# A recurrence, two attentions and a mixture of experts on one core: loads and splits reordered ahead of and in the recurrence, two pairs of padding memsets, a last chunk of 64 hidden rows

## The reference

```
x = x + attn(gru(cond, x))                    # x: [4, 256, 256]
x = x + ffn(adaln(x, cond))
gru:  r = sigmoid(x W_ih_r + h W_hh_r + b), z likewise, n = tanh(i_n + r * h_n)
      h = (1 - z) * n + z * h                 # 256 steps, batch 4, width 256
attn: 16 heads of width 128, causal           # W_q, W_k, W_v: 256 -> 2048
adaln: rms norm, scale and shift from cond @ W_emb; 16 heads of width 16 with
      rms norm of q and k by the gains g_q and g_k, no mask; o + o W_out
ffn:  16 experts of 176 hidden rows, the best 4 weighted, and one shared
      expert of 704 rows: silu(x W_gate) * (x W_up) @ W_down
```

## Time and profile before

| | us |
|---|---|
| median of 3 runs | 1003.25 (1001.9 to 1003.27) |
| the profiled execution | 1002.73 |
| its span | 1000.9 |
| busy: TensorE | 940.7 (94%) |
| VectorE | 694.6 (69%) |
| ScalarE | 593.7 (59%) |
| GpSimd | 581.4 (58%) |

### The profile page before, as it was taken

One profiled execution on the slowest core, in us unless ns is written; L12 is line 12 of the kernel. 1 busy time (PEld: TensorE's weight loads), 2 busy tenths in 40 slices (PEclk: granted clock), 3 DMA queues, 4 the chain that ended last, 5 costly groups with the idle time before them and its releaser, 6 DMA issues. The chain is left out here.

```text
span 1000.9 us, 37739 instructions
## 1 busy us (share of the span) xinstructions
PE 940.7 (94%) x15017; PEld 756.7 (76%) x15017; DVE 694.6 (69%) x2755; ACT 593.7 (59%) x2051; POOL 581.4 (58%) x1274
## 2 busy tenths in 40 slices
PE   3899999999999999998999999877999999999997
...
GB/s 370 47 15 24 25 25 25 20 19 25 25 25 24 20 19 25 25 32 96 72 73 72 73 127 41 21 41 1 2 2 5 60 134 112 111 125 118 125 112 44
DMA packets 79803, 58.99 MB, mean 59 GB/s; under 512 B 64886, under 2 KB 70776, under 8 KB 79116
## 3 DMA queue, kind: packets, MB, share of 16 engines
...
## 5 line engine op out<-in xcount | busy, mean ns | idle before, releaser
L577 POOL COPY gp<-hq 128x16 f16<-128x16 f16 x256 | 68.1, 266 | 152.8 <-DVE hq L541 152.7
L1988 PE MATMUL gu<-wq_part 128*128 128x512 f16 x660 | 151.5, 379 | 0.0
L617 POOL TENSOR_TENSOR q_part<-q_raw,q_part 128x64 f16<-128x64 f32 x237 | 113.1, 477 | 19.2
L352 PE MATMUL gq<-gp,wq_part 128*128 128x64 f16 x1422 | 120.6, 242 | 0.0
L280 PE MATMUL gr<-hq,w_one 128*128 128x4 f16 x2048 | 118.1, 166 | 0.0
L336 PE MATMUL gq<-gp,raws 128*128 128x64 f16 x1440 | 115.3, 237 | 0.0
L1988 PEld LDWEIGHTS gu<-wq_part 128*128 128x128 f16 x660 | 64.5, 98 | 66.5 <-issue 0.4
L2065 ACT ACTIVATE h_hi<-hT 128x512 f16<-128x512 f32 x56 | 35.3, 630 | 129.3 <-DVE hT L2135 129.3
L390 ACT ACTIVATE r_scan<-gr 128x8 f32<-128x8 f32 x256 | 46.1, 180 | 111.0 <-PE gr L280 110.9
L615 POOL CAST q_part<-q_raw 128x64 f16<-128x64 f32 x237 | 110.0, 464 | 0.4
L352 PEld LDWEIGHTS gq<-gp,wq_part 128*128 128x128 f16 x1422 | 94.5, 132 | 0.0
...
## 6 DMA issues: line engine op xcount, KB each, us to landing
...
```

The costliest lines, as they stand in the source:

```text
L352: mm = pe.matmul(q_bank[t % 2][:, 0:B * QB].rearrange("p (b t) -> p b t", b=B), wq_part[:, w, c, j * P:(j + 1) * P], gp[:, g, j, :, h * QB ...
L577: nc.gpsimd.tensor_copy(gp[:, :, :, :, t].rearrange("p q j b -> p q (j b)"), hq[:, nxt, :, 2::3]).then_inc(h_stored, 1)
L617: nc.gpsimd.tensor_tensor(q_part[:, 1, h, :, :, c], src, q_part[:, 0, h, :, :, c], ALU.subtract).then_inc(q_split, 1)
L1988: mm = pe.matmul(dst[:], w[:, c % 2, cols], y[:, j, halves[hf]], start=(n == 0), stop=(n == 3 * J - 1))
```

## The change

There are five edits.

1. Ahead of the recurrence SyncE loads x0, W_ih in three gates, W_hh, then as before. ScalarE's queue issues the start state and the bias rows. ScalarE and VectorE split W_hh gate by gate as well, the bias is scaled in one operation behind all three gates, and TensorE's input products go by gates with the first parts first. TensorE waits for each third of W_hh where it is used in t=0.
2. W_k's split on ScalarE and GpSimd begins at t=6 (`WK_AT`) instead of 1 and 2; what GpSimd does of W_q stays tied to it and so goes to t=11 to 19. VectorE's uses of both stay where they are.
3. The embedding products are made two a step at t=9 to 12.
4. The product of the gains is made at the end of the attention's GpSimd program. The padding is done in two pairs of memsets; the second waits until VectorE has scaled the two tiles.
5. In chunk 27 gate and up rows (64 each) stand in one set of weights: unit 54 makes 6 products into `GB` (tokens 0 to 511) and 6 into `UB` (tokens 512 to 1023), unit 55 none. The rest of h goes into the upper 64 rows of `h_hi`, opposite a copy of the down weights, so that 8 down products do a unit.

```diff
-EMB = 6
+EMB = 9
+WK_AT = 6
...
+            sp.dma_start(x0[:], dram["x0"]).then_inc(loaded["x0"], 16)
+            for g, name in enumerate(("wih_r", "wih_z", "wih_n")):
+                sp.dma_start(wih[:, :, gate_cols(g)], dram["wih"][:, :, gate_cols(g)]).then_inc(loaded[name], 16)
             sp.dma_start(whh[:], dram["whh"]).then_inc(loaded["whh"], 16)
-            sp.dma_start(x0[:], dram["x0"]).then_inc(loaded["x0"], 16)
-            sp.dma_start(wih[:], dram["wih"]).then_inc(loaded["wih"], 16)
-            sp.dma_start(condT[:], dram["condT"]).then_inc(loaded["cond"], 16)
-            sp.wait_ge(bias_zero, 1)
-            for row in (0, 32):
-                sp.dma_start(bias_raw[row:row + 2, :], dram["gru_bias"]).then_inc(loaded["bias"], 16)
             sp.dma_start(xT.rearrange("p j b t -> p j (b t)"), dram["xT"]).then_inc(loaded["xT"], 16)
...
-                j, (w, x) = k // 3, ((1, 0), (0, 0), (0, 1))[k % 3]
+                j, (w, x) = k % 2, ((0, 0), (0, 1), (1, 0))[k // 2]
...
-            places = [(g, k) for g in range(6) for k in range(6)] + [(g, 6) for g in range(8)]
+            places = [(2 * gate + mi, k) for gate in range(3) for k in range(6) for mi in range(2)] \
+                + [(g, 6) for g in range(8)]
...
+                if g % 2 == 0 and k == 0:
+                    pe.wait_ge(inputs_one, g // 2 + 2)
+                if (g, k) == (0, 2):
+                    pe.wait_ge(inputs_two, 1)
+                if g % 2 == 0 and k == 4:
+                    pe.wait_ge(inputs_two, g // 2 + 2)
...
-                if EMB <= t < EMB + 4 * J:
-                    c, j = (t - EMB) // J, (t - EMB) % J
-                    if t == EMB:
+                if EMB <= t < EMB + 4:
+                    c = t - EMB
+                    if c == 0:
                         pe.wait_ge(loaded["emb"], 48)
                         pe.wait_ge(loaded["cond"], 16)
-                    mm = pe.matmul(q_bank[0][:, c * B:(c + 1) * B], wemb[:, j, c * P:(c + 1) * P],
-                                   condT[:, j, :], start=(j == 0), stop=(j == J - 1))
-                    if t == EMB + 4 * J - 1:
+                    for j in range(J):
+                        mm = pe.matmul(q_bank[0][:, c * B:(c + 1) * B], wemb[:, j, c * P:(c + 1) * P],
+                                       condT[:, j, :], start=(j == 0), stop=(j == J - 1))
+                    if c == 3:
...
+            act.dma_start(condT[:], dram["condT"]).then_inc(loaded["cond"], 16)
             act.wait_ge(bias_one, 1)
             nc.scalar.activation(z_gate[:, 0:1], z_sum[:, 0:1], ACT.Sigmoid)
+            act.wait_ge(bias_zero, 1)
+            for row in (0, 32):
+                act.dma_start(bias_raw[row:row + 2, :], dram["gru_bias"]).then_inc(loaded["bias"], 16)
...
-            act.wait_ge(loaded["wih"], 16)
-            for g in range(3):
-                cols = slice(g * D, (g + 1) * D)
-                nc.scalar.activation(wih_part[:, 0, :, cols], wih[:, :, cols], ACT.Copy,
+            for g, name in enumerate(("wih_r", "wih_z", "wih_n")):
+                act.wait_ge(loaded[name], 16)
+                nc.scalar.activation(wih_part[:, 0, :, gate_cols(g)], wih[:, :, gate_cols(g)], ACT.Copy,
                                      scale=WS).then_inc(inputs_one, 1)
             act.wait_ge(loaded["whh"], 16)
-            nc.scalar.activation(flat(w_one[:]), flat(whh[:]), ACT.Copy,
-                                 scale=WS).then_inc(w_one_ready, 1)
+            for g in range(3):
+                nc.scalar.activation(w_one[:, :, gate_cols(g)], whh[:, :, gate_cols(g)], ACT.Copy,
+                                     scale=WS).then_inc(inputs_one, 1)
...
-                if 1 <= t < 1 + H1:
-                    if t == 1:
+                if WK_AT <= t < WK_AT + H1:
+                    if t == WK_AT:
                         act.wait_ge(loaded["wk"], 32)
-                        act.wait_ge(w_ready, 1)
-                        act.wait_ge(wih_ready, 4)
-                    nc.scalar.activation(wk_part[:, 0, t - 1], wk[:, t - 1], ACT.Copy,
+                        act.wait_ge(inputs_two, 7)
+                    nc.scalar.activation(wk_part[:, 0, t - WK_AT], wk[:, t - WK_AT], ACT.Copy,
...
-                if g == 0:
-                    dve.wait_ge(loaded["bias"], 32)
-                    dve.wait_ge(bias_zero, 2)
-                    for row in (0, 32):
-                        nc.vector.tensor_scalar(bias[row:row + 2, :], bias_raw[row:row + 2, :], WS, None,
-                                                ALU.mult).then_inc(bias_one, 1)
-            dve.wait_ge(bias_one, 3)
+                rest(wih_part[:, 1, :, cols], wih[:, :, cols], WS, wih_part[:, 0, :, cols]).then_inc(inputs_two, 1)
+            dve.wait_ge(loaded["bias"], 32)
+            dve.wait_ge(bias_zero, 2)
+            nc.vector.tensor_scalar(bias[0:34, :], bias_raw[:], WS, None, ALU.mult).then_inc(bias_one, 1)
+            dve.wait_ge(bias_one, 2)
             rest(bias[32:34, :], bias_raw[32:34, :], WS, bias[32:34, :]).then_inc(bias_ready, 1)
-            dve.wait_ge(w_one_ready, 1)
-            rest(flat(w_two[:]), flat(whh[:]), WS, flat(w_one[:])).then_inc(w_ready, 1)
+            for g in range(3):
+                cols = gate_cols(g)
+                dve.wait_ge(inputs_one, 5 + g)
+                rest(w_two[:, :, cols], whh[:, :, cols], WS, w_one[:, :, cols]).then_inc(inputs_two, 1)
...
-                if 2 <= t < 2 + H1:
-
-                    h, half = t // 2 - 1, slice(t % 2 * P, (t % 2 + 1) * P)
+                if WK_AT <= t < WK_AT + H1:
+
+                    h, half = (t - WK_AT) // 2, slice(t % 2 * P, (t % 2 + 1) * P)
...
+            pool.wait_ge(adaln["w_in"], 16 * len(ADALN_LOADS))
+            nc.gpsimd.tensor_tensor(adaln["gqk"][:, 0:D], adaln["gqk"][:, 0:D], adaln["gqk"][:, D:2 * D],
+                                    ALU.mult).then_inc(adaln["g_ready"], 1)
...
-            pool.wait_ge(w_in, 16 * len(ADALN_LOADS))
-            nc.gpsimd.tensor_tensor(g_both[:], gqk[:, 0:D], gqk[:, D:2 * D], ALU.mult).then_inc(g_ready, 1)
             nc.gpsimd.memset(q_rows[:, 0:TILES // 2, :, 3 * SLOT:], 0.0).then_inc(pads, 1)
+            nc.gpsimd.memset(k_rows[:, 0:TILES // 2, :, 3 * SLOT:], UNIT).then_inc(pads, 1)
             rest(1)
-            nc.gpsimd.memset(k_rows[:, 0:TILES // 2, :, 3 * SLOT:], UNIT).then_inc(pads, 1)
+            pool.wait_ge(xn_ready, 2 * TC)
             nc.gpsimd.memset(q_rows[:, TILES // 2:, :, 3 * SLOT:], 0.0).then_inc(pads, 1)
...
+                parts = ((h_hi, w_hi), (h_hi, w_lo), (h_lo, w_hi)) if c < NCH - 1 else ((h_hi, w_hi), (h_hi, w_lo))
                 for k in range(4):
                     i = 4 * hf + k
-                    for n, (h, w) in enumerate(((h_hi, w_hi), (h_hi, w_lo), (h_lo, w_hi))):
+                    for n, (h, w) in enumerate(parts):
...
+                if u == units - 2:
+                    pe.wait_ge(g_act, u)
+                    product(both[0], c, 0, 0, g_psum)
+                    pe.wait_ge(prod_ready, u)
+                    product(both[1], c, 0, 1, g_psum)
+                elif 0 < u < units - 2:
...
+                    nc.scalar.activation(act_g[u % 2][lower], both[u % 2][upper], ACT.Silu,
+                                         scale=1.0 / GS).then_inc(g_act, 1)
...
+                if 0 < u < units - 1:
+                    gated(u)
+                if u == units - 2:
+                    gated(u + 1)
...
+            def product(u):
+                rows, source = (slice(0, P), UB) if u < units - 2 else (lower, both[u % 2])
+                if u < units - 2:
+                    dve.wait_ge(u_psum, u + 1)
+                dve.wait_ge(g_act, u + 1)
+                nc.vector.tensor_tensor(prod[rows, u % 2, :], source[rows], act_g[u % 2][rows],
+                                        ALU.mult).then_inc(prod_ready, 1)
...
+                if u == units - 2:
+                    product(u + 1)
                 dve.wait_ge(hi_ready, u + 1)
-                nc.vector.scalar_tensor_tensor(out=h_lo[:, u % 2, :], in0=hT[:, u % 2, :],
-                                               scalar=HS / GS, in1=h_hi[:, u % 2, :], op0=ALU.mult,
+                second = h_lo[:, u % 2, :] if c < NCH - 1 else h_hi[upper, u % 2, :]
+                nc.vector.scalar_tensor_tensor(out=second, in0=hT[rows, u % 2, :],
+                                               scalar=HS / GS, in1=h_hi[rows, u % 2, :], op0=ALU.mult,
                                                op1=ALU.subtract).then_inc(lo_ready, 1)
...
+    gates, ups = hidden(gu[:, :INTER], sgu[:SHARED]), hidden(gu[:, INTER:], sgu[SHARED:])
+    gates[HID:], gates[HID - REST:HID] = gates[HID - REST:HID].copy(), ups[HID - REST:HID]
     down = hidden(w["L0_ffn_expert_down"].transpose(0, 2, 1), w["L0_ffn_shared_down"].T)
+    down[HID:] = down[HID - REST:HID]
```

91 lines of the change are left out of this document (47 added, 44 removed).

## The result

The changed kernel takes **997.13 us** (median of 6 runs, 996.53 to 998.43), the kernel before 1003.12 (1001.9 to 1003.27, 6 runs). The ratio is 0.9944, 95% interval 0.9933 to 0.9955: faster by 6.0 us, where 8.9 were forecast. The direction and the order of size were right, and the time lies just inside the low and high that I gave (991.6 to 997.4); by the ratio, though, it stands at 997.6, outside.

The account below looks back on a forecast made before the run. Bounds: TensorE and the last unit's way out at the end, VectorE's splits at the start, a stretched VectorE pair at the seam. Terms -2.8 - 4.3 + 0.6 - 2.4 = -8.9 gave 994.2 us, range 991.6 to 997.4.

Parts of the forecast that it names:

- Last chunk: End of the last stage: with fewer gate/up and down products the third output sum starts at 994.1, not 996.89: -2.8 us.
- Ahead of the recurrence: Kernel start: earlier loads and a shorter VectorE chain put the first n product at 10.5 or 10.6, not 14.90: -4.3 us.
- W_k's move: Recurrence, W_k's split from t=6: wait for W_k goes, -1.7; early steps -0.3 and +0.2; GpSimd delays VectorE at t=20, +1.6.
- Embedding: Recurrence, t=9 to 12: with two embedding products a step TensorE becomes the bound: +1.0 us (0 to +1.5).
- Padding: Seam between attention and adaptive norm: VectorE's scaling no longer waits across four GpSimd instructions: -2.4 us.
- The recurrence behind t=24: Later recurrence steps: no change forecast; a step other than 1.71 us from t=22 on would show the prediction wrong.
- Rival 2: Kernel start: bias rows or pieces of W_ih land late, the start gains only 2.5: 996.0 us, chance 0.12.
- Rival 1: Recurrence, t=20: GpSimd doesn't hold VectorE, the conversion is there in time; 1.6 less: 992.6 us, chance 0.15.
- Rival 3: Seam: second pair of memsets holds VectorE again, padding gains 1.0 or nothing: 995.6 to 996.7 us, chance 0.12.
- Rival 4: Recurrence: wait for W_k becomes a wait for GpSimd's backlog, +3 instead of +0.6: 996.6 us, chance 0.10.
- Rival 5: Recurrence: idleness at t=20 halves TensorE's clock and it stays there; slower than before, 1007 us at eight steps, chance 0.03.

Follow-up runs that it names:

- the run with the heads early: Changed kernel, but GpSimd makes the first parts of W_q's heads 11 to 15 at t=3 to 7, not t=11 to 19: 996.12 us, ratio 0.9937.
- the one with two memsets: Changed kernel with two tiny memsets of a tile nobody reads added at the start of VectorE's program: 996.07 us, ratio 0.9927.

## Why the prediction was wrong, step by step

- **Last chunk** (-2.8; -2.48 in the trace): right. To the third output sum it is 2.84 less; the other 0.36 is that the four sums now follow one another and their transfers come later behind them. 64 partitions cost as much as 128 (0.68 against 0.69), as assumed, and reading the upper half into the lower cost nothing.
- **Ahead of the recurrence** (-4.3, bounds -4.6 and -2.5; -1.44, and -1.8 as the mean of eight traces): this is the step that failed. It said "by the same rate (404 KB a us) the gates land at about 4.1, 4.7 and 5.3, and W_hh at 7.3". The gates came at 4.81, 5.38 and 7.16 and W_hh at 10.81. The rate was that of other transfers, 307 GB/s came instead, and the bound of -2.5 did not cover it, as it varied only the bias rows, which were in time (5.66). With W_hh at 9 to 11, whatever VectorE saved was no longer on the path. I had costed the instructions and taken the loads as given, where the edit moved the loads.
- **W_k's move** (-1.7, -0.3, +0.2, +1.6; -1.79, -0.36, and +1.45 at t=18 to 24): right in place, and the run with the heads early shows the cause of two thirds of it. The size is in part luck. The 1.6 were all to be the wait for head 15's conversion; that was 0.97, and the 0.48 beside it stood in the forecast only as a bound. W_k was to land at 20.0 and be asked for at 21.7, with 1.7 to spare; it landed at 23.21, and no wait came only because the start had gained so little that ScalarE asked at 24.61.
- **Embedding** (+1.0; +0.93): right, by the same reason.
- **Padding** (-2.4; -2.46): right, and the run with the memsets in a row shows it. Behind the seam 0.35 went again in the profiled pair. From GpSimd's first cast to the last stage's first product eight of the 17 traces show 101.06 to 101.11 and nine, the profiled pair among them, 101.65 to 102.02. The nine are just those in which the granted clock stood at half for 3.4 us, 34 to 36 us behind that cast, and there TensorE's transposes of 128 columns fall behind. The same 3.4 us in the changed kernel and in the one with two memsets (busy us and count of PE, PEld, DVE, ACT, POOL, then clock, DMA):

```profile
698.50:701.90 3.40, 3.17 (x28) 2.53 (x28) 2.12 (x6) 2.03 (x3) 3.32 (x6) 0.50 0.00 0
```

```profile
697.03:700.43 3.40, 2.73 (x40) 2.07 (x40) 3.07 (x7) 2.61 (x4) 3.32 (x6) 1.00 0.00 0
```

28 products against 40. So the 0.35 are no price of the padding: both traces lose to this stretch, the one of before 0.6 and the changed one 0.9. Why the clock falls in some executions and not in others stays open: TensorE's idle times ahead of the stretch, 1.21 and 1.40, are the same in all 17.
- **The recurrence behind t=24** (nothing; +1.34): a term that the sum did not have. The prediction did name the sign of it, that "the recurrence from t=22 on were no longer 1.71 a step", and the other one, that the last stage starts less than 5 us earlier (1.84): both came.
- **Rivals.** Rival 2 (996.0) came true in its place, the start, by the pieces of W_ih and with them W_hh, not by the bias rows; with the recurrence's 1.3 on top, which it did not have, it gives 997.3. Rivals 1, 3 and 4 did not come: VectorE waited 1.12 at t=20, the padding gained its 2.4, and W_k's move cost no more than its sum. Rival 5 has to be struck, below. The chance I gave the forecast, 0.48, took the loads' landing for settled.

Without the two misses (2.5 at the mean start, 1.3 behind t=24) the forecast's 8.9 would be 5.1; measured were 6.0. The 0.9 between is within what single stretches vary from execution to execution: 1.4 at the start, 0.96 in the adaptive norm.
